# Local attention: window masks as pairs of 64-row bf16 products, and another order of the steps

## The reference, cut to what matters

```python
sim = jnp.einsum('bhwid,bhwjd->bhwij', bq, bk)      # bq has the factor 8
mask = (i < j) | (i > j + WINDOW) | (j == -1)
sim = jnp.where(mask, -jnp.finfo(sim.dtype).max, sim)
attn = jax.nn.softmax(sim, axis=-1)
out = jnp.einsum('bhwij,bhwjd->bhwid', attn, bv)
```

## Time and profile before

| | us |
|---|---|
| median of 3 runs | 2175.29 (2173.99 to 2176.82) |
| profiled execution, device time | 2170.47 |
| its span | 2168.9 |
| TensorE matmuls busy | 1899.3 (88%), 13304 instructions |
| VectorE busy | 1183.1 (55%) |
| ScalarE busy | 975.3 (45%) |
| GpSimd busy | 859.6 (40%) |
| masks of the second scores, L960 | 256 matmuls, 0.384 each |

### The profile page before, as it was taken

The page is one execution under the profiler, slowest core; times in us unless marked ns, Lnnn a source line. Parts: engine busy times, 40 slices in busy tenths (PEclk is TensorE's granted clock), DMA queues, the critical chain, the costliest instruction groups (busy, mean ns, idle before and its releaser), DMA issues. The chain is left out here.

```text
span 2168.9 us, 41374 instructions
## 1 busy us (share of the span) xinstructions
PE 1899.3 (88%) x13304; PEld 1430.2 (66%) x13304; DVE 1183.1 (55%) x3145; ACT 975.3 (45%) x1962; POOL 859.6 (40%) x790
## 2 busy tenths in 40 slices
PE   4999999999955999999996999579999999778887
PEld 2666566656634677777765888557777777667776
DVE  3566566556626676666632333376666777234443
ACT  1455555555523555555543344235555555333332
POOL 4132332223213555555531333145555555224334
PEclk8899999999967999999996999799999999979998
DMA  4535543454211000000002211300000000022221
GB/s 107 108 80 96 107 107 82 84 112 103 48 54 36 11 29 29 29 29 29 19 20 79 68 58 48 108 11 30 28 6 23 29 29 19 30 89 77 71 73 41
DMA packets 100550, 121.25 MB, mean 56 GB/s; under 512 B 20186, under 2 KB 72596, under 8 KB 100500
## 3 DMA queue, kind: packets, MB, share of 16 engines
q1 hardware_dynamic: 93588, 95.44, 18.5%
q0 software_dynamic: 6912, 25.17, 3.0%
HBM read 82.55 MB, written 37.77 MB: 55 GB/s over the span
## 5 line engine op out<-in xcount | busy, mean ns | idle before, releaser
L390 DVE TENSOR_REDUCE a_negm<-a_x 128x1 f32<-128x128 f32 (+3 forms) x512 | 240.8, 484 | 205.8 <-PE a_x L481 200.8
L362 ACT ACTIVATE a_PT<-a_c 128x512 f32<-128x512 f32 (+3 forms) x512 | 219.7, 437 | 241.9 <-PE a_c L501 234.9
L671 POOL TENSOR_TENSOR l_t<-l_t 128x512 f32<-128x512 f32 x128 | 164.3, 1284 | 219.8 <-DVE l_t L816 217.6
L479 PE MATMUL a_x<-a_K,a_Q 96*128 96x256 f32 (+2 forms) x512 | 214.8, 423 | 34.7 <-DMA a_K<-qk_parts 19.8
L499 PE MATMUL a_c<-a_Q,a_K 97*128 97x256 f32 (+2 forms) x512 | 210.9, 418 | 7.7 <-ACT a_PT L362 7.4
L834 DVE CUSTOM_DVE_ANT_0 l_x<-l_x,window 128x256 f32<-128x256 f32 (+1 forms) x512 | 184.5, 422 | 45.4 <-PE l_x L924 43.9
L1276 DVE SCALAR_TENSOR_TENSOR m_hid<-m_a,m_b,m_gate 128x512 f32<-128x512 f32 x96 | 71.9, 749 | 244.8 <-ACT m_gate L1199 221.3
L858 PE MATMUL l_f<-l_w_hi,l_xt_hi 128*128 128x512 f32 x384 | 172.0, 448 | 34.4 <-DVE l_xt_lo L793 24.7
L746 ACT ACTIVATE l_PT<-l_c 128x512 f32<-128x512 f32 (+1 forms) x256 | 124.5, 538 | 79.0 <-PE l_c L960 79.0
L1144 POOL TENSOR_TENSOR m_hid_lo<-m_hid,m_hid_hi 128x512 fp32r<-128x512 f32 x80 | 102.5, 1288 | 144.5 <-ACT m_hid_hi L1210 144.3
L860 PE MATMUL l_f<-l_w_lo,l_xt_hi 128*128 128x512 f32 x384 | 152.7, 398 | 0.0
(11 more groups left out here) (236 smaller groups left out, 5182.6 us busy)
## 6 DMA issues: line engine op xcount, KB each, us to landing
a_Q<-qk_parts SPq DMA_DIRECT2D x96, 128.0 KB, 4.0
a_K<-qk_parts SPq DMA_DIRECT2D x96, 128.0 KB, 5.1
qk_parts<-a_qk_hi SPq DMA_DIRECT2D x32, 256.0 KB, 2.1
qk_parts<-a_qk_lo SPq DMA_DIRECT2D x32, 256.0 KB, 2.1
after_attn<-l_out POOLq DMA_DIRECT2D x16, 512.0 KB, 5.3
m_h<-after_attn SPq DMA_DIRECT2D x32, 256.0 KB, 2.9
m_xr<-after_attn SPq DMA_DIRECT2D x16, 512.0 KB, 4.1
a_xin<-in_L_attn_x SPq DMA_DIRECT2D x8, 512.0 KB, 3.5
```

The lines of the kernel that those rows point to most:

```text
L362: nc.scalar.activation(PT[:, h // HP % 2, h % HP, QOFF[j]:QOFF[j] + nq], SC[i % 2][:, q0:q0 + nq], ACT.Exp, scale=AD ** -0.5)\
L390: dve.tensor_reduce(negm[:, q, h:h + 1], MX[i % 2][:, 0:P * (q + 1)], AX.X, ALU.max, negate=True).then_inc(max_done, 1)
L479: pe.matmul(r[:, 0:nk], Q[0:MROW, h, P * q:P * q + P], Kk[0:MROW, h, 0:nk], start=True, stop=True)
L671: pool.tensor_tensor(t1[:, par, w, :], t1[:, par, w, :], t2[:, par, w, :], ALU.add)\
```

## The change

The mask of a step is computed as eight products instead of two. Each takes 64 rows of a mask table as weights, and 64 rows of the identity as columns, read twice so that both key blocks of the step (t = 0, 1) get it: 128 columns. Head 0 uses the row half 0 to 63 and head 1 the half 64 to 127. Since a row half of `window` holds the mask of 64 queries only, a second table, `window_sw`, holds the same mask with its halves exchanged; `n` picks the table and, with `hh ^ n`, the queries. The identity is no longer the weights. The signal to ScalarE comes with the last product of each head. `constants` makes one more table, so MADE is 20. And the list of the steps has another order, with the same steps.

```diff
-MADE = 15
+MADE = 20
@@ constants
+        "window_sw": sb("window_sw", [P, 2, P], BF16),
...
-            pool.wait_ge(made, 7)
+            pool.memset(k["window_sw"][:, :, :], 0.0).then_inc(made, 1)
+            pool.wait_ge(made, 8)
...
+            for at in (0, P // 2):
+
+                pool.wait_ge(made, MADE - 4 + 4 * at // P)
+                m = k["window_sw"][at:at + P // 2]
+                pool.affine_select(out=m[:, 0, :], in_=m[:, 0, :], compare_op=ALU.is_ge, fill=NEG, base=at - P // 2,
+                                   pattern=[[1, P]], channel_multiplier=-1).then_inc(made, 1)
+                pool.affine_select(out=m[:, 1, :], in_=m[:, 1, :], compare_op=ALU.is_ge, fill=NEG, base=P // 2 - at,
+                                   pattern=[[-1, P]], channel_multiplier=1).then_inc(made, 1)
@@ local_attention, STEPS
-            f_x:0 f_xe:0 sm:4 st:0 f_qk:0 sm:5 f_qe:0 st:1 ps:0 f_qk:1 f_qe:1 f_iv:0 sm:6 st:2 f_qk:2 pv:0 f_qk:3
-            f_qe:2 sv:0 f_qe:3 z:0 sm:7 st:3 ps:1 f_qk:4 f_iv:1 f_qe:4 f_qk:5 xr:0 mt:1 f_qe:5 f_iv:2 st:4 f_qk:6
-            f_qk:7 pv:1 zn:0 f_qe:6 f_qe:7 f_iv:3 st:5 sv:1 ps:2 z:1 st:6 pv:2 zn:1 zs:0 f_t:0 zs:1 f_te:0 sv:2
-            f_sm:0 z:2 f_t:1 zn:2 f_te:1 st:7 f_sm:1 f_t:2 f_te:2 ps:3 pv:3 zs:2 f_sm:2 f_t:3 sv:3 f_te:3 z:3 f_sm:3
-            f_v:0 zn:3 f_v:1 zs:3 f_v:2 f_mt:0 f_v:3 out:0""".split()]
+            sm:4 f_x:0 f_xe:0 st:0 sm:5 f_qk:0 f_qe:0 st:1 f_qk:1 ps:0 f_qe:1 f_qk:2 f_iv:0 sm:6 f_qe:2 st:2 f_qk:3
+            f_qe:3 sm:7 f_iv:1 pv:0 f_qk:4 f_qe:4 sv:0 z:0 st:3 f_qk:5 ps:1 f_qe:5 mt:1 zn:0 f_qk:6 f_iv:2 f_qe:6
+            st:4 f_qk:7 f_qe:7 f_iv:3 pv:1 st:5 sv:1 z:1 ps:2 zs:0 st:6 zn:1 pv:2 xr:0 f_t:0 f_t:1 f_te:0 f_sm:0
+            f_te:1 sv:2 z:2 zn:2 st:7 ps:3 f_sm:1 f_t:2 pv:3 zs:1 f_te:2 f_sm:2 zs:2 f_t:3 f_te:3 sv:3 f_sm:3 z:3
+            zn:3 f_v:0 f_v:1 zs:3 f_mt:0 f_v:2 f_v:3 out:0""".split()]
@@ local_attention, TensorE, step st
-                        mask = K["window_t"][:, :, :].rearrange("p b q -> p (b q)").unsqueeze(1).to_broadcast([P, 2, 2 * P])
-                        for hh in range(2):
-                            pe.matmul(SC[hh][:, :].rearrange("p (t q) -> p t q", t=2), K["identb"][:, :], mask,
-                                      start=False, stop=True, skip_group_check=True).then_inc(sc_full, 1)
+                        for n, table in enumerate((K["window"], K["window_sw"])):
+                            for blk in range(2):
+                                for hh in range(2):
+                                    rows, at = slice(FD * hh, FD * hh + FD), FD * (hh ^ n)
+                                    m = pe.matmul(SC[hh][:, :].rearrange("p (t b q) -> p t b q", t=2, b=2)
+                                                  [:, :, blk, at:at + FD], table[rows, 1 - blk, :],
+                                                  K["identb"][rows, FD * hh:FD * hh + FD].unsqueeze(1)
+                                                  .to_broadcast([FD, 2, FD]), start=False, stop=True,
+                                                  skip_group_check=True)
+                                    if n == 1 and blk == 1:
+                                        m.then_inc(sc_full, 1)
```

## The result

The changed kernel takes 2203.25 us (median of 4 runs, 2200.55 to 2208.03); the kernel before took 2174.64 beside it (4 runs). The ratio is 1.0144, with a 95% interval of 1.0106 to 1.0182: slower, by 29 us. The forecast was 2200.

What follows compares the result with a forecast made beforehand. TensorE, busy 88% of the span, sets the pass. 14 passes at +2.0 us, +1.4 for constants and -3.5 for tails give +26; with 2170.5 and 4.8 that is 2201, said as 2200; range 2162 to 2228.

Steps and rivals of the forecast that it cites:

- Masks: Masks of a score step on TensorE: eight 64-row products in side-by-side pairs take 0.26 us instead of 0.54.
- Changes of form: TensorE switching between 128-row and 64-row matmuls: 0.20 us each, six more a pass (+1.2 us), +0.06 twice at `sm`.
- Steps 3 to 5: `f_qk:3` and `f_qk:7`: VectorE's tiny maximum L812 waits for GpSimd's `ps`; new TensorE waits of 1.33 and 1.24 us.
- Step 6: At `mt:1`, now followed by `f_qk:6`: the 0.7 us wait for the copied maxima goes, 0.75 with restart.
- Step 7: At `pv:2`, only the shorter `st:6` stands between it and `sv:1`: wait 0.80 us instead of 0.52.
- Step 8: `f_t:1` right behind `f_t:0` waits for its banks (l_QL, l_KL): 1.36 us; the 0.63 wait for l_KL and 0.08 go.
- Step 1: Start of the pass: VectorE does the maxima of `sm:4` ahead of xt_lo, a wait of 0.16 us.
- Constants: Making the table `window_sw` on GpSimd before all else: +1.4 us.
- Tails: The two tails, where score steps wait for exponentials: steps end earlier at seven places, -1.75 us each, -3.5 together.
- The first batches' front part: Part without `ps` and with the same GpSimd order: no change in time taken.
- L812 slipped in ahead of `ps`: Rival: the maximum waits only for the earlier sum; both places 2165 us (chance 0.14), only the second 2184 (one slip 0.12).
- The clock: Rival: TensorE's clock falls to 1.2 GHz in the loop near `pv:2` and `f_t:1`; in every pass, 2225 us; chance 0.08.

Runs made afterwards that it cites:

- kernel 3: The changed kernel with `ps:0` moved behind `f_qe:1` and `ps:1` behind `f_qe:5`; 2162.84 us (one run), a pass of 56.70; timed again, ratio 0.9964.
- kernel 4: The changed kernel without the maximum over 128x16 and VectorE's wait in front of it; 2168.87 us (one run), a pass of 56.71.
- kernel 8: Kernel 3 with head 0's four mask products in each step issued twice, 12 products instead of 8; 2193.53 us (one run), a pass of 57.96.
- kernel 5: Kernel 3 with `st:7` moved between `f_t:0` and `f_t:1`, and `f_te:0` moved up; 2174.86 us (one run), a pass of 56.71.
- 1: The new masks alone, in the order of the kernel before; 2168.18 us against 2176.39, ratio 0.9957.
- 9: New masks in the old order, its middle rearranged: `f_qk:4` ahead of `st:3`, `f_qk:6` ahead of `st:4`, some others moved; 2168.69 us against 2179.53, ratio 0.9951.
- kernel 7: Kernel 3 with each step's eight masks issued head by head, four of head 0 then four of head 1; 2172.1 us (one run), a pass of 56.74.

## Why the prediction was right, point by point

The time (2200 for 2203.25) and the mechanism in the loop were right, and with them the named places; one step outside the loop failed.

- *Masks.* 0.26 us a step forecast, 0.24 measured; pairs 0.055 us apart, as the profile was said to show. By the 81 ns for each product of the Trainium skill (TensorE: Matmul & The Clock Gate, Back-to-back issue gap), an estimate, it would have been 0.65; no run here shows that for these 64-row products.
- *Changes of form.* +0.20 where a projection follows a mask: it takes 1.59 instead of 1.39 us from end to end, in all places without a wait; +0.06 for `sm` behind a mask in the same form (0.297 against 0.24). Taking the prolongations by waits (4.93 us, next points) from 59.17 leaves 54.2 us of bare array time, where 54.5 was forecast.
- *Steps 3 to 5, L812.* Forecast 1.33 and 1.24 us for `f_qk:3` and `f_qk:7`, lasting 1.4 and 1.5 us; measured, with the restart, 1.23 and 1.21, lasting 1.54 and 1.58. Kernel 3 moves one partner of the meeting away and kernel 4 leaves the other out, and both take the two waits away. This is shown, and it is the whole of the loss: without it the change is faster than before (0.9964).
- *Step 6.* The wait for l_mrow went. *Step 7*, `pv:2`: 0.80 forecast, 0.81 measured. *Step 8*, `f_t:1`: 1.36 and 1.36. *Step 1*, xt_lo: 0.16 forecast, 0.32 measured, the one term off by half.
- *A pass* was forecast 2.0 us longer and is 1.8; the 14 come to 23.6 us instead of 28, since the first of each layer loses only 1.05. *Constants*: 1.4 forecast; TensorE's first transposes start at 12.71 us instead of 11.20, 1.5 later. *Tails*: -1.75 each forecast, -2.6 and -2.3 measured; TensorE is also 3.4 us less at 1.2 GHz (0.50) in each, so not all of this need be the steps.
- *The first batches' front part* was the step that failed. "The first batches' front part has no ps and the same GpSimd order; I take nothing." From its `f_x` to the next it is 2.3 us longer in the first layer and 1.4 in the second. Of each, 0.44 is only where the line is drawn: the `sm:4` of a pass now stands ahead of `f_x` (so there is one less behind the last `f_x`, which the figures of the tails allow for). What is left is 1.9 and 1.0 us. Waits of TensorE explain little of it: those of `f_sm` for negm (0.4 to 1.6 us in the first layer) and of `f_t:1` for l_QL (0 to 0.7) rose, since here too `f_t:1` stands directly behind `f_t:0`, and that for l_KL (1.4) went; its idle time as a whole is 0.5 us more in the first layer and 0.4 less in the second. The rest is TensorE's busy time, 1.3 and 1.4 us more without that `sm:4`, for the same work, more of which now falls where the clock is low: in the second layer it stands at 1.2 GHz (0.50) for 31.7 us instead of 27.8, and for the first it is shown below the list.
- *Rivals.* L812 slipped in ahead of `ps` at neither place. The clock stayed at 1.00 in the loop, through 0.73 us of idle ahead of `pv:2` and 0.98 behind the transposes that follow it, so the doubt about it was not borne out. The masks ran side by side.
- *Chances.* The named outcomes slower than before add to 0.77, where the prediction says 0.70.

The four projections `f_v` at the end of the first layer's front part, before and after (columns as in the earlier trace rows; the granted clock is the 0.98 and the 0.80):

```profile
699.42:705.64 6.22, 6.22 (x31) 5.08 (x30) 2.24 (x9) 2.29 (x4) 0.00 (x0) 0.98 0.00 0
706.24:713.84 7.60, 7.60 (x30) 5.87 (x28) 2.24 (x9) 2.28 (x4) 0.00 (x0) 0.80 0.00 0
```

TensorE never idles in either, and the same projections take 1.4 us more. A stretch at granted clock 0.50, that is 1.2 GHz, ends 0.3 us into them before and 3.1 us into them after. In kernels 4 and 8, with the same order here, they run at 1.00 and take 6.19 us, but begin later, at 53.7 and 54.5 us after `f_x` instead of 52.9, so that the front is hardly shorter there, 60.3 and 61.1 us. That the front is longer belongs to the order, since it showed in all kernels that have it; what moves the clock's rise and fall against the steps, no run tests. The clock was weighed as a rival for the loop alone.

The sum over the profiled executions: passes +23.6, front parts +2.9, tails -4.9, constants +1.5, together +23.1 of the 30.1. The other 7.0 lie in code that is the same: 4.8 in the first attention and 2.2 behind the tails. The local attention began at 647.0 us before and at 653.3 after, and in the other kernels with the same constants anywhere from 649.7 (kernel 3) to 659.8 (kernel 8). The granted clock goes with it: from the first transpose to the first `f_x` of the local attention TensorE is at 1.2 GHz for 101 us of 637 in kernel 3 and for 128 of 646 in kernel 5; before it is 108 of 636 and after 111 of 641. Over all twelve profiled executions a microsecond more at 1.2 GHz goes with about 0.46 more of length, an estimate by a straight line through them, so 3.5 us of it would be 1.6 of the 4.8. The code behind the tails varies the same way (33.6 us at 1.2 GHz before and 36.6 after, behind the first of them). So this part is not shown to be the change's, and that the total came within 3 us of the forecast is partly luck: a step put at nothing cost 2.9, the same code elsewhere 7.0, while the passes were taken 4.4 and the tails 1.4 too dear.

What stays open: why the clock falls at other places in code that is the same, which no run tested. And five kernels with the new masks (1, 3, 4, 5 and 9) all end at 56.6 to 56.7 us a pass, each with 1.5 to 2 us of waits, in different places. Whether an order without them exists was not found.

## What to carry to other kernels

An instruction's own duration is the place to look for one engine holding up another: where a tiny VectorE operation is long at times and always ends with a GpSimd instruction, its place in the order is worth more than its work. Time the two halves of a change apart before judging either: here one saved 8 to 9 us and the other, over two positions in a list, lost 35. A wait that is covered by moving a step comes back elsewhere unless the moved step's own inputs are early: of three attempts here one gained nothing, one lost 0.6 us and one won 0.1 us a pass.

## What the runs showed of the hardware that was not expected

- The two row halves of TensorE don't keep to the program's order between each other. With four 64-row products of one half issued ahead of four of the other (kernel 7), products of the second group started ahead of some of the first, in pairs 0.006 to 0.008 us apart, and eight still took 0.245 us. The head is inferred there, but kernel 8 has a `window_sw` started ahead of a `window` that precedes it in the program. With eight on one half and four on the other (kernel 8) the eight alone set the time, 0.46 us at 0.056 each.
- A bf16 product of 64 rows and 128 columns keeps its row half for 0.055 us although its own weights are loaded for each one; the weight load is longer (0.094 us in its records) and overlaps the products before it.
- The meeting of VectorE's maximum and GpSimd holds against a 1.83 us instruction as against one of 1.27: 1.54 and 1.58 us instead of the 0.17 that the same instruction takes with GpSimd idle (kernel 3).
